# Second quantisation of layer 0 kept in the channel layout, a new order at the entry of attention, and split projections in a two-layer cross-attention and feed-forward kernel

## The reference

```
x = x + cross_attention_0(layernorm(x), ctx)      # 16 heads of 64
x = x + ffn_0(layernorm(x))                       # quantised, with a convolution
x = x + cross_attention_1(layernorm(x), ctx)      # 16 heads of 16, rms norm, rope
x = x + ffn_1(layernorm(x))                       # scales taken over all batches

def act_quant(x):                                 # layer 0, one scale for each token
    scale = 127.0 / clip(max(abs(x), axis=-1), 1e-05)
    return clip(round(x * scale), -128, 127) / scale
ffn_0: h = act_quant(x) @ ternary(w1).T ; h = silu(conv3_over_tokens(h) + b)
       return act_quant(h) @ ternary(w2).T        # the second quantisation, 1024 channels
```

## Time and profile before

| | before |
|---|---|
| median of 3 runs | 2503.68 us (2501.91 to 2503.96) |
| profiled execution | 2504.27 us |
| its span, first to last instruction | 2502.5 us |
| PE busy | 2395.5 us, 96% |
| DVE, ACT, POOL busy | 69%, 64%, 64% |
| mean granted clock of PE | 0.987 |

### The profile page before, as it was taken

How to read it: one execution, slowest core, us unless ns; L and a number is a source line. 1 busy time by engine, 2 the same in 40 slices (tenths; PEclk the granted TensorE clock), 3 DMA queues, 4 the chain that set the end, 5 groups by cost and what they waited for, 6 DMA issues and landing times.

```text
span 2502.5 us, 59414 instructions
## 1 busy us (share of the span) xinstructions
PE 2395.5 (96%) x18926; PEld 1789.6 (72%) x18926; DVE 1716.0 (69%) x4475; ACT 1594.5 (64%) x4337; POOL 1595.0 (64%) x1846
## 2 busy tenths in 40 slices
PE   7999999999999999999999999999999999999567
PEld 5777777777777777777777777777777777777336
DVE  6666666676666667766666676666667666666777
ACT  4666666766666667666666766666676666666446
POOL 2666676666667766666776666667666666776506
PEclk9999999999999999999999999999999999999689
DMA  4000000000000000000000000000000000000202
GB/s 154 27 10 10 10 8 10 2 10 10 10 10 10 8 4 8 10 10 10 10 8 7 4 10 10 10 10 8 10 2 10 10 10 10 10 2 3 53 8 60
DMA packets 34524, 37.02 MB, mean 15 GB/s; under 512 B 2804, under 2 KB 32964, under 8 KB 34500
## 3 DMA queue, kind: packets, MB, share of 16 engines
q1 hardware_dynamic: 34500, 36.71, 4.9%
HBM read 29.36 MB, written 7.34 MB: 15 GB/s over the span
## 4 chain that ended last, share of the span: by engine, by line
PE 75%; DVE 10%; issue 5%; ACT 5%; POOL 4%; DMA 0%; ACTq 0%; DVEq 0%; SPq 0%; POOLq 0%
PE pt L409 16%; PE ps L330 16%; PE ps L399 14%; PE pa L421 7%; PE pa L456 5%; PE ps L383 5%; DVE z L1130 4%; PE pa L436 4%; POOL prob L1403 2%; ACT prob L755 2%; DVE nmx L984 1%; POOL qrs L1446 1%; PE ps L649 1%; PE pt L553 1%; PE ps L449 1%
## 5 line engine op out<-in xcount | busy, mean ns | idle before, releaser
L984 DVE TENSOR_REDUCE nmx<-ps 112x2 f32<-112x750 f32 x512 | 479.7, 937 | 199.8 <-PE ps L399 199.7
L1403 POOL TENSOR_TENSOR prob<-prob,rinv 112x375 f32<-112x375 f32 x512 | 405.7, 814 | 222.5 <-DVE rinv L1000 216.5
L1403 POOL TENSOR_TENSOR f1w_room<-f1w_room,rinv 112x375 f32<-112x375 f32 x512 | 404.6, 815 | 63.3 <-DVE rinv L1000 54.8
L716 ACT ACTIVATE room<-ps 128x375 f32<-128x375 f32 (+2 forms) x480 | 228.0, 488 | 290.5 <-PE ps L330 290.5
L975 DVE COPY probT<-pt 125x336 f32<-125x336 f32 x512 | 254.1, 496 | 116.2 <-PE pt L409 116.2
L716 ACT ACTIVATE probT<-pt 125x336 f32<-125x336 f32 x512 | 231.4, 452 | 118.0 <-PE pt L409 114.9
L409 PEld LDWEIGHTS pt<-ident,prob 112*125 112x125 f32 x1536 | 190.9, 189 | 129.6 <-issue 69.5
L409 PEld LDWEIGHTS pt<-ident,f1w_room 112*125 112x125 f32 x1536 | 196.7, 187 | 119.0 <-issue 54.4
L1426 POOL TENSOR_TENSOR krs<-krs,nhalf 125x48 f32<-125x48 f32 x32 | 257.0, 8031 | 0.0
L399 PE MATMUL ps<-kT,q 64*112 64x375 f32 x1024 | 230.5, 528 | 17.0 <-ACT f1w_room L755 14.6
L409 PE MATMUL pt<-ident,f1w_room 112*125 112x112 f32 x1536 | 238.0, 286 | 2.6 <-DVE probT L975 1.3
(11 more groups left out here) (261 smaller groups left out, 5164.6 us busy)
## 6 DMA issues: line engine op xcount, KB each, us to landing
ctok<-in_ctx SPq DMA_DIRECT2D x32, 375.0 KB
xin<-in_x SPq DMA_DIRECT2D x32, 112.0 KB, 2.0
x_rows<-x SPq DMA_DIRECT2D x32, 112.0 KB, 1.9
out<-probT SPq DMA_DIRECT2D x8, 448.0 KB, 3.2
room<-x_rows SPq DMA_DIRECT2D x1, 2576.0 KB, 14.2
stage<-in_f1w SPq DMA_DIRECT2D x2, 1024.0 KB, 5.2
stage<-in_wk SPq DMA_DIRECT2D x1, 1024.0 KB, 8.5
stage<-in_wv SPq DMA_DIRECT2D x1, 1024.0 KB, 10.7
```

What stands on the lines that cost most here:

```text
L716: return act.activation(dst, src, ACT.Copy)
L984: top = dve.tensor_reduce(nmx[:, g:g + 2], ps[0:T, 2 * (i % 2):2 * (i % 2) + 2, 0:S], AX_X, ALU.max, negate=True)
L1403: pool.tensor_tensor(prob(i, n), prob(i, n), rinv[:, g:g + 1].to_broadcast([T, S]), ALU.mult).then_inc(s["normed"], 1)
```

## The change

1. *Second quantisation.* y stays in the channel layout. After each half DVE reduces |y| over the four chunks, per partition and token, into `amx` [128, 2, 112]. PE turns the two slices of `amx`; DVE takes the largest over 256 columns, forms 1/scale, and a diagonal matrix; PE multiplies ones with it, so each partition has the token scales in PSUM; DVE multiplies y with them and rounds straight into `hqT`. ACT's part, `hr`, `hq` and all sixteen turns go. POOL's scaling of the keys waits for `amx_ready` in place of `y_ready`.
2. *LEAD = 4*: the loop's attention takes four pairs of layer 0 first, then the eight of layer 1, then four of layer 0. POOL's roots of q alternate with pairs 2 to 5.
3. *Entry order.* v0 piece 4 moves ahead of the turn of `xn`; the turn of q (`query_turn`) moves behind scores 2; DVE's masks and squares, ACT's copies of q and v0 piece 5's copy move into the first steps of attention.
4. *Split projections.* K piece 4 is cut 3 + 3 around the turn of `xq` and the scale's product, V piece 3 is cut 4 + 2 around the product with `f0w2`, Q half 0 is cut 3 + 1 quarters around the new scale's product.
5. *Tail.* In the first pass DVE rounds the next chunk's rows ahead of this chunk's maxima (but for the first). In the second, POOL's adds and the stores go by half chunks with semaphores of their own.

```diff
-DVE_STEPS = 29
+DVE_STEPS = 32
+        LEAD = 4
-            if i < AHEAD:
+            if i < LEAD:
                 return 0, i
-            return (1, i - AHEAD) if i < AHEAD + PAIRS else (0, i - PAIRS)
+            return (1, i - LEAD) if i < LEAD + PAIRS else (0, i - PAIRS)
...
-                    k0_proj(b + 1, range(0, 5), True)
+                    k0_proj(b + 1, range(0, 4), True)
+                    pe.wait_ge(s["k0_sb"], b * IC + (IC + 1))
+                    k0_terms(4, 0, 3)
...
                 pe.matmul(pa[:, 1, 0:T], ones[0:T, :], diag[:], start=True, stop=True).then_inc(s["rb_ready"], 1)
+                if not last_batch:
+                    k0_terms(4, 3).then_inc(s["k0_ready"], 1)
...
-                for j in range(FC):
-                    if j % HT == 0:
-                        pe.wait_ge(s["y_ready"], b * 2 + (j // HT + 1))
-                    last = pe.transpose(pa[0:T, j // HT, (j % HT) * P:(j % HT + 1) * P], th[:, j, :], ident[:])
...
                     x0_transpose(b + 1)
                     v0_proj(b + 1, [2])
-                    q0_proj(b + 1, 0)
-                for j in range(FC):
-                    if j % HT == 0:
-                        pe.wait_ge(s["hq_ready"], b * 2 + (j // HT + 1))
-                    last = pe.transpose((pt_b0, pt_b1)[j // HT][:, (j % HT) * T:(j % HT + 1) * T],
-                                        hq[:, j * P:(j + 1) * P], identb[0:T, 0:T])
...
+                pe.wait_ge(s["amx_ready"], b * 2 + 2)
+                for n in range(2):
+                    last = pe.transpose(pt[0:T, 1, n * P:(n + 1) * P], amx[:, n, :], ident[:])
+                last.then_inc(s["amT_ready"], 1)
+                if not last_batch:
+                    q0_proj(b + 1, 0, range(0, HT - 1))
+                pe.wait_ge(s["diag2_ready"], b + 1)
+                pe.matmul(pt[:, 1, 2 * P:2 * P + T], ones[0:T, :], diag[:], start=True, stop=True)\
+                    .then_inc(s["rb2_ready"], 1)
+                if not last_batch:
+                    q0_proj(b + 1, 0, range(HT - 1, HT))
...
+                if not last_batch:
+                    pe.wait_ge(s["v0_sb"], b * 6 + 9)
+                    v0_terms(3, 0, 4)
...
-                    v0_proj(b + 1, [3])
+                    v0_terms(3, 4).then_inc(s["v0_ready"], 1)
                     q0_proj(b + 1, 1)
+                    v0_proj(b + 1, [4])
...
                     if part == MIDDLE and i == 0:
+                        query_turn(b)
                         pe.wait_ge(s["q1_sq"], b + 1)
                         v0_proj(b + 1, [5])
                     if part == MIDDLE and i == 1:
+                        pe.wait_ge(s["q1_sb"], b + 1)
...
                         exps(i + AHEAD, part, b)
+                        if part == MIDDLE and i == 0:
+                            v0_copy(b + 1, [5])
+                        if part == MIDDLE and i == 2:
+                            query_copies(b)
...
+                    link(dve.scalar_tensor_tensor(flat(th)[:, half], flat(th)[:, half], 1.0, flat(z)[:, half], ALU.add,
+                                                  ALU.mult))
+                    dve.tensor_reduce(amx[:, n, :], th[:, chunks, :].rearrange("p j t -> p t j"), AX_X, ALU.max,
+                                      apply_absolute_value=True).then_inc(s["amx_ready"], 1)
+
+                dve.wait_ge(s["amT_ready"], b + 1)
+                link(dve.tensor_reduce(am[:, 6:7], pt[0:T, 1, 0:2 * P], AX_X, ALU.max))
+                link(dve.tensor_scalar(am[:, 3:4], am[:, 6:7], 2 * A8_EPS, 1.0 / 127.0, ALU.max, ALU.mult))
+                link(dve.reciprocal(am[:, 4:5], am[:, 3:4]))
+                dve.tensor_scalar(diag[:], ident[0:T, 0:T], am[:, 4:5], None, ALU.mult).then_inc(s["diag2_ready"], 1)
+                dve.wait_ge(s["rb2_ready"], b + 1)
+                for n in range(2):
+                    chunks = slice(HT * n, HT * n + HT)
+                    link(dve.tensor_tensor(th[:, chunks, :], th[:, chunks, :],
+                                           pt[:, 1, 2 * P:2 * P + T].unsqueeze(1).to_broadcast([P, HT, T]), ALU.mult))
+                    dve.tensor_scalar(hqT[:, chunks, :], th[:, chunks, :], ROUND, ROUND, ALU.add, ALU.subtract)\
+                        .then_inc(s["hqT_sb"], 1)
...
+                    if part == MIDDLE and i == 0:
+                        query_masks(b)
                     if i + 1 < count:
                         row_sum(i + 1, part, b)
+                    if part == MIDDLE and i == 0:
+                        query_squares(b)
...
+                if 0 < c < NCH - 1:
+                    next_rows(c)
                 largest(c, 0)
                 largest(c, 1)
...
-                pool.wait_ge(s["y_ready"], b * 2 + 2)
+                pool.wait_ge(s["amx_ready"], b * 2 + 2)
...
-                    attention(MIDDLE, b, 0, 1)
+                    attention(MIDDLE, b, 0, 2)
...
+                    for n in range(4):
+                        query_root(n)
+                        attention(part, b, n + 2, n + 3)
+                    attention(part, b, 6, G)
...
+                for n in range(2):
+                    half = slice(2 * n, 2 * n + 2)
...
+                    pool.tensor_tensor(outc[:, half, :], scaled[:, half, :], x3n[:, half, :], ALU.add)\
+                        .then_inc(s["o3_sum"], 1)
```

More of the change, by code:

```diff
@@ L162, in xattn_ffn_kernel @@
         diag = sb("diag", [T, T])
+        amx = sb("amx", [P, 2, T])
         rb = sb("rb", [P, T])
@@ L317, in _, with exact3 @@
             with sp.Fori(0, NCH) as c:
-                sp.wait_ge(s["o3_sum"], c + 2)
-                sp.dma_start(out_rows[c], outc).then_inc(s["o3_out"], 16)
-            sp.wait_ge(s["o3_out"], 16 * NCH + 16)
+                for n in range(2):
+                    sp.wait_ge(s["o3_sum"], c * 2 + (n + 3))
+                    sp.dma_start(out_rows[c][:, 2 * n:2 * n + 2, :], outc[:, 2 * n:2 * n + 2, :])\
+                        .then_inc(s[("o3_low", "o3_high")[n]], 16)
+            sp.wait_ge(s["o3_low"], 16 * NCH + 16)
+            sp.wait_ge(s["o3_high"], 16 * NCH + 16)
         @block.tensor
         def _(pe):
-            def exact3(dst, left, right, more=None):
-                terms = [(l, r, c) for l, r in ((1, 0), (0, 1), (0, 0)) for c in range(DC)]
-                for n, (l, r, c) in enumerate(terms):
-                    last = pe.matmul(dst, left(l, c), right(r, c), start=(n == 0), stop=(n == len(terms) - 1))
+            TERMS = [(l, r, c) for l, r in ((1, 0), (0, 1), (0, 0)) for c in range(DC)]
+            def exact3(dst, left, right, first=0, end=len(TERMS)):
+                for n, (l, r, c) in list(enumerate(TERMS))[first:end]:
+                    last = pe.matmul(dst, left(l, c), right(r, c), start=(n == 0), stop=(n == len(TERMS) - 1))
                 return last
@@ L375, in x0_transpose, with q0_proj @@
                 last.then_inc(s["xT0_ready"], 1)
-            def q0_proj(k, g):
-                pe.wait_ge(s["v0_sb"], k * 6 + (g + 1))
-                pe.wait_ge(s["xT0_sb"], k + 1)
-                for j in range(HT):
+            def q0_proj(k, g, quarters=range(HT)):
+                if 0 in quarters:
+                    pe.wait_ge(s["v0_sb"], k * 6 + (g + 1))
+                    pe.wait_ge(s["xT0_sb"], k + 1)
+                for j in quarters:
                     for c in range(DC):
@@ L458, in wo0_product, with query_turn @@
                     last.then_inc(s["wo_ready"], 1)
+            def query_turn(b):
+                pe.wait_ge(s["q1_rope"], b + 1)
+                for c in range(DC):
+                    last = pe.transpose((pt[:, 0], pa[:, 1])[c][:, 0:T], q1b[:, c * P:(c + 1) * P], ident[0:T, 0:T])
+                last.then_inc(s["q1T_ready"], 1)
             def attention(part, b):
@@ L474, in attention @@
                         turn(i - 1, part, b)
-                    if part == MIDDLE and i == AHEAD + 1:
+                    if part == MIDDLE and i == 3:
                         pe.wait_ge(s["v0_sb"], b * 6 + 12)
@@ L769, in attention @@
                 for i in range(count):
-                    if part == MIDDLE and i == AHEAD + PAIRS + 2:
+                    if part == MIDDLE and i == LEAD + PAIRS + 2:
                         o1_copy(part, b)
@@ L788, in attention, with query_copies @@
                     o1_copy(part, b)
+            def query_copies(b):
+                act.wait_ge(s["q1T_ready"], b + 1)
+                for m in range(4):
+                    ins = act.activation(q1[:, 1, m, :], pa[:, 1, 0:T], ACT.Copy, scale=mask1[:, m:m + 1])
+                ins.then_inc(s["q1_sb_act"], 1)
             def o1_copy(part, b):
-                act.wait_ge(s["pv"], at(PAIRS + (AHEAD if part == MIDDLE else 0), part, b))
+                act.wait_ge(s["pv"], at(PAIRS + (LEAD if part == MIDDLE else 0), part, b))
                 copy(oT1[:], pa[:, 1, 0:DC * T].rearrange("p (j t) -> p j t", j=DC)).then_inc(s["o_sb"], 1)
@@ L821, in rest @@
```

(15 more changed lines are left out.)

120 lines of the change are left out of this document (53 added, 67 removed), and 1 row of the table names.

## The result

The changed kernel takes 2482.77 us (median of four runs, 2479.49 to 2486.74) against 2503.82 of the kernel before in the same session (2501.91 to 2504.75): a ratio of 0.9918, 95% interval 0.990 to 0.9935. That is 21 us less where 45.5 were forecast: inside the range, outside the likeliest case. The profiled execution took 2484.45 us, its span is 2482.6.

What follows compares the result with a forecast made beforehand. PE, busy 96% of the span, was taken to bound the kernel, mostly in 31 loop turns. Loop 37 us, last batch -0.7, first pass 4, output 5: 45.5 us less, 2458 us; likeliest 2444 to 2474, range 2430 to 2492.

Steps and rivals of the forecast that it cites:

- work ledger: Cross-check of one loop turn: 0.9 us of PE work out, pauses of 2.4 closed, new pauses of 2.0.
- pause (c): PE from the turn of `xn` to the fifth pair's scores: 8.1 us of work in 9.4, so 1.3 of pauses.
- K projection split: Three K matmuls after the scale's product fill a PE pause; the first feed-forward product starts 0.36 us earlier.
- pause (a): PE between the turn of `xq` and the first feed-forward product: some 0.35 to 0.4 of 0.73 us is a pause.
- slower: Rival, chance 0.13: the reduction over permuted `th` at a third of the rate (1.55 us) gives 2517 us.
- longer chain: Rival, chance 0.18: POOL's `xbo` gets the ports first, `diag` ends 0.75 us later each turn; 2481 us.
- `diag` behind POOL's keys: In the new scale's chain, DVE's `diag` waits until POOL has scaled the keys: 0.25 us more PE pause a turn.
- Entry order: Start of the loop's attention: a new 0.8 us wait for pair 0's exponentials, yet scores 4 start 1.0 us earlier.
- Four pairs ahead: Loop's attention: pauses of 0.4 to 0.5 us mostly go, scores 7 wait 0.3 for ACT; net gain 0.2 a turn.
- pauses (d): First eight attention steps: some turns of a pair take 0.97 instead of 0.84 us; an estimated 0.4 us of pauses.
- Last batch: Nothing covers its chain; x2 stands behind DVE's weight scaling of 2.7 us: an estimated 0.7 us lost.
- Tail: After the loop: layer 1's first feed-forward pass gains 4 us over 6 chunks, output in halves 5 us.

Runs made afterwards that it cites:

- u1_quant: Changed kernel with the second quantisation of before put back (eight turns of `th`, eight of `hq`): turn 72.056 us, time 2487.94 us, ratio 0.9936.
- u3_ksplit: Changed kernel with the fifth K projection in one piece again, ahead of the turn of `xq`: turn 72.072 us, time 2490.16 us, ratio 0.9948.
- e1_near: Changed kernel with each reduction group made of four neighbours (wrong channels, durations of a real reduction): turn 71.196 us, time 2460.67 us, ratio 0.9819.
- e3_one: Changed kernel with one reduction over all eight chunks in place of two, and one turn instead of two: turn 71.936 us, time 2484.86 us, ratio 0.9919.
- e9_turned: Changed kernel with y written so that a token's four chunks lie side by side: turn 72.091 us, time 2487.83 us, ratio 0.9942.
- u2_entry: Changed kernel with the entry order of before put back, two pairs ahead instead of four: turn 72.674 us, time 2506.82 us, ratio 1.0018.
- e6_qlate: Changed kernel with ACT's four masked copies of q1 moved from attention step 2 to step 4: turn 72.070 us, time 2487.17 us, ratio 0.9936.
- e7_pad: Changed kernel with one float of room behind each row of `th` (step 452 bytes, not 448): turn 71.833 us, time 2479.35 us, ratio 0.9904.

## Where the prediction held and where it failed

*What bounds it.* Right: turns of the loop carry the time, and PE's pauses decide. The work ledger held: PE's busy time in a turn fell by 1.3 us (1.03 of it goes with the quantisation, by u1_quant; the rest was not separated). In pause (c) a sum was wrong: its terms make 8.3 us of work, not 8.1, so 1.1 of pauses and not 1.3, which the forecast didn't use. And the total as printed makes 45.3; the 45.5 takes the loop at 37.2.

*K projection split.* The size was off: 0.24 in place of 0.36. I had put the two small turns and the small product at 0.35; in the changed kernel they and three K matmuls (0.51) fill 12.12 to 13.11 us of the turn without a pause, so they take 0.48, and pause (a) was 0.25. u3_ksplit shows that all of it counts.

*The reductions, the step that failed.* "The nearest rows reduce 256 elements in 0.41 and 750 in 0.94, so 448 take 0.61." Those rows read neighbours; this one reads each group of four with steps of 448 bytes and takes 0.95, 1.7 ns an element. e1_near restores 0.62 and with it 0.64 us a turn, 19 us in all, and the turn lands on the forecast (71.20, forecast 71.2). The rival "slower" had the mechanism and the price right, 2 (t - 0.6), and named the missing row; its size, a third of the rate, was too hard, and 0.13 for it too little for a row that did not exist. The time fell on the sum of the rival "longer chain" (2481) by chance: `xbo` ahead of `diag` was not seen in any turn.

*The wait for `amx`.* Forecast 0.6, measured 1.2; with near groups 0.6 (visible 0.41). Right but for the reductions.

*`diag` behind POOL's keys.* Forecast 0.25 of extra pause; in the changed kernel none. The mechanism exists, with that size, in e3_one; here `diag` starts 0.21 us before the keys' end and loses nothing. A gain of 0.25 a turn over my sum.

*`hqT`.* No wait, as forecast; e9_turned shows how thin the room is: 0.17 us more per rounding was a wait.

*`xn`.* "Ready near 1034.6 as before", 29.6 us in the turn: it was ready at 30.25. It follows the f0w2 product by 3.64 to 3.70 us, and that product came 0.6 later. Covered by v0 4, so it cost nothing, but for the wrong reason in my text; without the new order it costs 0.66 (u2_entry).

*Entry order.* The wait for pair 0's exponentials came (0.46 visible, 0.5 to 0.8 in all). Scores 4 start 38.87 us in the turn instead of 39.43: 0.56 gained where 1.0 was forecast, which is the reductions' and the split's loss less the gain at `diag`.

*Four pairs ahead.* 0.2 forecast, nothing came where the traces can show it: from scores 4 to the next wo1 product it is 32.92 before and 32.96 after. Turns of a pair that take 0.96 or more instead of 0.84 are still there, three in a turn before (0.96 to 1.11) and four after (0.97 to 1.02); so the new order of POOL's roots did not remove the pauses (d). e6_qlate shows one of the four, the 1.02 ahead of scores 7, to be ACT's copies; the others stay open.

Sum of a turn: 1.2 - 0.12 - 0.64 + 0.25 - 0.2 = 0.49, measured 0.53.

*Last batch.* A loss of 0.7 forecast, 3.8 in the profile. The turn of `xn` is 1.6 us later in it than before: DVE's weight scaling (a reduction of 2.29 us and two small steps) used to end 0.9 before the product that x2 waits for, and is now the last thing ahead of x2, and the slow reductions stand ahead of it. The other 2.2 are the moment at which the granted clock came back (61 us in the turn, 54 before), and so no lasting cost of the change: in e7_pad it came at 52, and the turn took 66.56. I had not looked at the clock: in the kernel before it is down for this stretch as well.

*Tail.* Right. From rounding to rounding a chunk takes 4.6 us, forecast 4.7, before 5.39; 3.65 us in all, forecast 4:

```profile
2392.55 0.68 DVE L1335 TENSOR_SCALAR hq<-hr 112x1024 bf16<-112x1024 f32 x1
...
2397.14 0.68 DVE L1335 TENSOR_SCALAR hq<-hr 112x1024 bf16<-112x1024 f32 x1
...
2475.43 0.69 DVE L1388 TENSOR_TENSOR prob<-pa,th 112x512 f32<-112x512 f32 x1 [1.05 <-PE pa L709]
...
2475.73 1.26 POOL L1516 TENSOR_TENSOR probT<-prob,hr 112x512 f32<-112x512 f32 x1 [0.25 <-POOL hr L1511]
...
2478.43 1.26 POOL L1516 TENSOR_TENSOR probT<-prob,hr 112x512 f32<-112x512 f32 x1 [0.22 <-POOL hr L1511]
```

The output gave 5.5 against 5, but by another split. The last add ends at 2479.7, 3.6 after the last scaling at 2476.1, where 1.4 was forecast: a whole pair of POOL's operations for the last half still follows the first half's. Against 4.4 before that is 0.8, not 3; the other 4.7 came ahead of it, where a chunk takes 6.52 us instead of 7.06; for that I had put 2.

## What to carry to other kernels

Price an instruction by a row with the same access, not the same count: a permuted view of float32 data cost this DVE half as much again (0.95 us against 0.62 for 448 elements), on the reading or on the writing side, and combining whole rows avoids it (here for maxima without magnitudes). Where no such row exists, that term is the widest of the sum and should carry the chances. When work is moved ahead of a product, look at what was the cover of the chain behind it: here two thirds of a V piece moved ahead of the product open a wait of 0.66 us unless another filler comes behind it. A stretch in which PE idles can be paid twice, the second time in the clock of the next busy stretch, and that part moves from run to run: compare kernels by a stretch that repeats.

## What the runs showed of the hardware

- DVE, float32, 128 partitions: a reduction of 448 elements takes 620 ns over neighbours, 907 to 991 (mean 950) with steps of 448 bytes, 907 to 1006 (mean 954) with 452, and 896 elements 1682 ns with 448. Writing with a 16-byte step costs the three-operand instruction 969 instead of 615 ns; a rounding to bf16 that reads with it 565 instead of 394.
- A DVE tensor_scalar that starts 0.45 us before the end of a POOL instruction lasts 0.53 instead of 0.28, and POOL's next one doesn't hold it further (e3_one, 31 turns); starting 0.21 before the end it lasts its usual 0.28 (changed kernel). Both end 0.06 to 0.08 after POOL's instruction.
- The granted clock fell from 2.4 to 1.2 GHz in the last turn, where PE was busy 2.6 and then 0.7 of ten us, and came back 8 to 19 us into the closing attention, in which PE was busy 9.9 of ten, at a moment that differed by 9 us between two kernels with the same instructions there. Useless matmuls in the waits kept it up for all but some 7 us.
